# Landing times of the experts' weight loads and stores in a planner's table: a hybrid attention and mixture-of-experts kernel

## The reference

```python
gate_scores = jax.nn.softmax(jnp.einsum('btd,de->bte', x, Wg) + bg, axis=-1)
top1_idx = jnp.argmax(gate_scores, axis=-1)
top1_mask = jax.nn.one_hot(top1_idx, NUM_EXPERTS, dtype=x.dtype)
top1_weight = jnp.sum(gate_scores * top1_mask, axis=-1, keepdims=True)
h = jax.nn.silu(jnp.einsum('btd,edh->bteh', x, W1) + b1)
o = jnp.einsum('bteh,ehd->bted', h, W2) + b2
y = jnp.sum(o * top1_mask[..., None], axis=2) * top1_weight
...
x = x + _L0_attn_a_ref(_layernorm(x, axis=-1), ...)
x = x + _L0_ffn_ref(_layernorm(x, axis=-1), ...)
x = x + _L0_attn_b_ref(_layernorm(x, axis=-1), ...)
x = x + _L0_ffn_ref(_layernorm(x, axis=-1), ...)
```

## Time and profile before

| | |
|---|---|
| time, median of 3 | 1585.77 us |
| lowest and highest | 1582.77, 1590.88 us |
| profiled execution | 1582.86 us |
| its span, first to last instruction | 1581.1 us |
| instructions | 26957 |
| TensorE, VectorE, ScalarE, GpSimd busy | 88%, 75%, 69%, 45% |
| matmuls of the sums (L1253) | 16 records, from 99.3 to 254.5 us |

### The profile page before, as it was taken

One profiled execution on the slowest core, in us unless ns is written; L12 is line 12 of the kernel. 1 busy time (PEld: TensorE's weight loads), 2 busy tenths in 40 slices (PEclk: granted clock), 3 DMA queues, 4 the chain that ended last, 5 costly groups with the idle time before them and its releaser, 6 DMA issues.

```text
span 1581.1 us, 26957 instructions
## 1 busy us (share of the span) xinstructions
PE 1399.3 (88%) x9196; PEld 592.6 (37%) x9196; DVE 1179.1 (75%) x1997; ACT 1083.7 (69%) x1788; POOL 704.9 (45%) x770
## 2 busy tenths in 40 slices
PE   3987999999999999889999999889888889999937
PEld 1322333334555333255442323223222234454436
DVE  4765878877777778757778887888888997678324
ACT  1554666666666677668787887787786877778812
POOL 3410434323332664468665465351432015766633
PEclk7998999999999999789999999999999999999969
DMA  6675755875772324777411220210202116534222
GB/s 192 189 247 163 218 158 173 250 219 150 207 217 60 97 67 157 234 222 233 153 49 35 61 81 21 70 33 25 84 21 60 43 63 213 176 113 145 84 101 82
DMA packets 126909, 204.21 MB, mean 129 GB/s; under 512 B 16616, under 2 KB 92034, under 8 KB 126774
## 3 DMA queue, kind: packets, MB, share of 16 engines
q1 hardware_dynamic: 117464, 188.15, 39.6%
q0 software_dynamic: 6016, 12.71, 2.4%
q10 hardware_dynamic: 3294, 1.64, 0.4%
HBM read 127.33 MB, written 76.53 MB: 129 GB/s over the span
## 4 chain that ended last, share of the span: by engine, by line
PE 60%; DVE 10%; POOL 9%; ACT 6%; DMA 6%; issue 5%; SPq 2%; ACTq 0%; POOLq 0%; DVEq 0%
PE ps L1164 17%; PE ps L1130 11%; PE ps L1151 10%; DVE Mb L1478 6%; PE ps L1245 5%; PE ps L1260 5%; ACT P L1354 4%; PE ps L1098 4%; POOL ROW L1422 4%; PE ps L1172 2%; POOL rs L1700 2%; DMA TH<-in_b 2%; DMA X<-xs 1%; PE ps L1198 1%; PE ps L1114 1%
## 5 line engine op out<-in xcount | busy, mean ns | idle before, releaser
L1478 DVE TENSOR_REDUCE Mb<-ps 128x2 f32<-128x1024 f32 (+1 forms) x951 | 938.6, 1014 | 228.6 <-PE ps L1130 221.4
L1354 ACT ACTIVATE P<-ps 128x512 f32<-128x512 f32 (+1 forms) x1070 | 805.8, 784 | 258.3 <-PE ps L1151 242.3
L1130 PE MATMUL ps<-STK 32*128 32x512 f16 (+1 forms) x1536 | 412.1, 389 | 45.1 <-DMA STK<-qka 16.3
L1151 PE MATMUL ps<-STK 32*128 32x512 f16 (+1 forms) x1536 | 416.8, 388 | 28.2 <-ACT P L1354 13.8
L1164 PE MATMUL ps<-P,V 128*32 128x512 f32 x3072 | 416.9, 615 | 4.6 <-ACT P L1354 4.1
L1130 PEld LDWEIGHTS ps<-STK 32*128 32x128 f16 (+1 forms) x1536 | 103.8, 94 | 293.3 <-DVE Mb L1478 96.1
L1151 PEld LDWEIGHTS ps<-STK 32*128 32x128 f16 (+1 forms) x1536 | 107.6, 94 | 253.8 <-issue 77.3
L1745 POOL DMA_INDIRECT xs<-ROW,slot x64 | 63.3, 989 | 105.6 <-DVE slot L1568 90.5
L1752 POOL TENSOR_TENSOR TH<-TH,Z 128x512 f32<-128x512 f32 x58 | 73.8, 1273 | 73.7 <-ACT Z L1402 73.1
L1164 PEld LDWEIGHTS ps<-P,V 128*32 128x32 f32 x3072 | 61.0, 109 | 118.9 <-issue 101.8
L1245 PE MATMUL ps<-XT,WE 128*128 128x128 f32 x696 | 98.8, 287 | 3.2 <-DVE Mb L1478 2.3
(11 more groups left out here) (156 smaller groups left out, 1395.6 us busy)
## 6 DMA issues: line engine op xcount, KB each, us to landing
WE<-wx SPq DMA_DIRECT2D x87, 576.0 KB, 4.2
STK<-qka SPq DMA_DIRECT2D x62, 480.0 KB, 6.3
qka<-HL SPq DMA_DIRECT2D x96, 256.0 KB
STK<-qkb SPq DMA_DIRECT2D x64, 256.0 KB, 2.7
qkb<-HL SPq DMA_DIRECT2D x96, 128.0 KB
X<-xs SPq DMA_DIRECT2D x77, 129.5 KB, 3.0
xs<-pad SPq DMA_DIRECT2D x8, 1036.0 KB, 8.6
qka<-HL SPq DMA_DIRECT2D x48, 128.0 KB
```

Source lines behind the costliest of these rows:

```text
L1130: mm = eng.matmul(ps[:, bank + i, :], l_, r_, start=True, stop=True)
L1151: mm = eng.matmul(ps[:, bank + i, :], l_, r_, start=True, stop=True)
L1354: eng.activation(P[:, st % 3, j:j + n, :], ps[:, bank:bank + n, :], ACT.Exp, scale=SCALE_A if g < 4 * B else SCALE_B).then_inc(sem("exp"), 1)
L1478: eng.tensor_reduce(Mb[:, g % 2, at:at + 4 * n - 3:4], ps[:, bank:bank + n, :], AX, ALU.max).then_inc(sem("mx"), 1)
```

## The change

Two figures in the table of landings: `wload` from 5 to 14, `wstore` from 5 to 8.

```diff
 LANDS = {"xload": 4.0, "setup": 3.0, "put": 3.0, "stack": 3.0, "mput": 2.0, "weights": 5.0, "rows": 3.8, "blank": 6.0, "weights_b": 4.0,
-         "weights_p": 3.0, "wload": 5.0, "wstore": 5.0, "scatter": 4.0, "fill": 5.0, "send": 4.0}
+         "weights_p": 3.0, "wload": 14.0, "wstore": 8.0, "scatter": 4.0, "fill": 5.0, "send": 4.0}
```

## The result

The changed kernel took 1604.17 us, the median of four executions from 1589.7 to 1610.41; before, now of four executions as well, took 1585.38 (1582.77 to 1590.88). The ratio is 1.0098, with a 95% interval from 1.0061 to 1.0136; that of the two medians is 1.012. So a difference was measured where none was forecast, and the time lies 11 us above the range. The profiled execution took 1605.21 us.

The account below looks back on a forecast made before the run. TensorE's queue, busy 88% of the span, was taken as the bound. The two figures' costs, 0 + 0, left the old median of 1585.8 us as the forecast, with a range of 1579 to 1593.

Parts of the forecast that it names:

- The edits cost nothing: Planner's table: neither landing figure changes any order, instruction or wait; cost 0 + 0; chance of no change 0.93.
- The first rival: Weight sums at L1253 move back behind about 9 us of other work; 17.5 us saved, 1568 to 1574; chance 0.01.
- the 3.5 us for slow matmuls: Half-clock matmuls at the second and third sums, saved if the stalls go; 3.5 us of the 17.5.
- The second, the late stores: Later sums delay weight stores, so the first expert's weights come 25.6 us late; 1594 to 1611 us; chance 0.01.
- each sum's delay adds to the last store's: At the eight sums: each 9 us further back, moving the last store by 72 us.
- The rival's own remark: Weight loads stand 22 us apart on average, which would swallow most of the 9 us.
- The forecast of the median from three executions, and the range: Whole kernel: median 1585.8 us, range 1579 to 1593, from the times seen and some 3 us beyond each end.
- the third rival: Whole kernel: same program measured over 0.5% (7.9 us) off; chance 0.02 below 1577, 0.03 above 1594.
- The rule on the clock: TensorE's clock gate: slow matmul count varies from run to run, below 1% of the span, up to 15.8 us.
- My sentence that a median should stand nearer than that: Whole kernel: a median of several executions should differ by less than the clock rule's 15.8 us.

Follow-up runs that it names:

- the version that does it: Changed kernel (landings 14 and 8) with the planner's sum made to wait for the load's landing, against before: ratio 0.9868, median 1576.08 us.
- the three repeats: Changed kernel unedited, twice, and the kernel before unedited, once, each against before: medians 1589.19, 1597.15 and 1591.72 us.
- the better plan with 40: Planner waiting for landings (14 and 8), plus ten throwaway transposes ahead of each of four layer-norm waits, against before: 0.9805, median 1557.76 us.
- the control: Kernel before with ten throwaway transposes at L1206 in batches 9, 11 and 13, where TensorE hardly idles: ratio 0.9994, median 1602.11 us.
- the version with 9 and 5: Kernel before with the planner's sum waiting for the load's landing, landings 9 for load and 5 for store: ratio 0.9946, median 1582.92 us.

## Why the prediction was wrong

**The edits cost nothing: right.** No reader of the two figures was overlooked, the lists are the same, the waits at L1253 are 16.3 us in three pieces against the 15 or so foretold, with 10.65 before the third sum.

**The first rival, that the change does what it says: right as a price, and not this change.** It was put at 17.5 us, or two thirds of that; the version that does it gained 13.4 of the median, 0.9916. One term was a little high: the pair of L1253 was priced against 0.86 us at full clock, a row of the chain, where TensorE's order of time has 1.02 for the same pair (217.24), so that the 3.5 us for slow matmuls were 0.3 too much. **The second, the late stores: wrong** even there. The step that failed in it is that each sum's delay adds to the last store's. Where the planner listens, the sums stand some 20 us apart, from 111 to 251 us, the last one 3 us sooner than before, and the last store stays at 255. The rival's own remark that loads 22 us apart would swallow most of the 9 us was the better half of it.

**The forecast of the median from three executions, and the range: here it failed.** "I take both ends for the range and a little more" sized the scatter of one program's times at -0.4% and +0.5%. It was 2.3% from end to end in 97 executions, and only 39 of these lie inside 1579 to 1593. The median of the 97 is 1596.5. The four executions of before that I had seen lie below it, three of the four of the change above. Which set fell to which side is luck or the occasion; nothing on record tells which. The time measured, 1604.17, is the third rival, "the same program, measured apart", above 1594. It had 0.03. Of the 97 executions 57 are at 1594 or above.

**The rule on the clock was weighed, and thrown out too early.** A wider range could have been argued from the profile, though not how wide. The rows of before show idles of TensorE and the half clock behind them, and the rest of that trace has more such idles, like that of batch 12. Behind the one at batch 12 the lower clock was short or long, by the execution. I took the clock's 0.963 as a property of the kernel, when it was one draw of 0.936 to 0.968. The Trainium skill (TensorE: Matmul & The Clock Gate, Part 1: The HAM clock gate (the "warmup" mystery)) says that the number of slow matmuls differs from run to run of one kernel. The runs agree: from 1190 to 1270 us the granted clock was 0.70 to 0.98 in five of them. It also puts the cost of the ramp at below 1% of a typical span. What varied here is more than a ramp at the start, and it is larger: the times are 2.3% apart from end to end, and 1.2% between the medians of the lowest and the highest set of four or more (1585.38 and 1604.17). My sentence that a median should stand nearer than that was the step in which the range went wrong: a median of four inherits its set, and the sets differ.

**And the interval.** 1.0061 to 1.0136 leaves out 1, for a program against itself. It is made from the scatter within the two sets, and doesn't know what differs between them. With the kernels side by side on one chip, the three repeats gave 0.9983, 0.9994 and 1.0029, each with 1 inside its interval.

## What to carry to other kernels

Before costing an edit to a planner's table, follow the figure to its reader: here the landing time was written down and never asked for, and the one line that asks for it was worth 0.8% of the median with the landing time at 14. A new plan moves other waits too, so add up all waits of the engine, and not only those that the edit was for. Look at the granted clock of both profiles before any other difference, and where it differs take no time to be the edit's until the old kernel has run beside the new one. Where TensorE stands idle for 1 to 2 us in a stretch that is otherwise dense, throwaway matmuls ahead of the wait can pay: 30 of them took 0.4 to 0.6% off this kernel, and the better plan with 40 stood at 1557.8 in the median, where before beside it stood at 1593.0.

## What the runs showed of the hardware

- After an idle of 1.5 us at one place TensorE's clock stayed at 1.2 GHz for some 4 us in one execution and for 48 us in two others of the same program, although it was busy for 92% of the time there (in the profile after). What ends such a stretch, and what of it depends on the chip, stays open: before had a median clock of 0.960, 0.956 and 0.950 on three chips.
- The clock also fell behind shorter waits: some 30 us at 1.2 GHz in the control between 1054 and 1094 us, among waits of 0.2 to 0.7 us.
- At 1.2 GHz a kernel with TensorE at 89% slows VectorE and ScalarE with it: in 40 us VectorE was busy for 26.1 instead of 37.5.
- The start differs too: the first scores (L1130) began at 36.22 us before, behind an idle of 15.46, and at 39.00 after, behind 17.56, with the same DMAs ahead of them.
- One execution of the version with 9 and 5 took 1790.69 us at a granted clock of 0.732; its eleven others lie between 1574.13 and 1598.13. I have no profile of it.
